# ScalarE's row statistics of tile i+2: behind the transposes of tile i+1, or ahead of the first gelu half of tile i

## The chip, the cores and the metric

The kernel runs on one core of one Trainium2 chip. The metric is the device time of one execution in microseconds. The kernel before was timed three times: 1892.87, 1883.16 and 1890.80 us, median 1890.8 us.

## What is computed

A transformer layer over `x` of 16 sequences x 512 tokens x 256 features, in float32, with three parts that are summed:

```python
xn = layernorm(x)
a  = xn + gdn(layernorm(xn, ln1))          # gated delta rule: a recurrence over the 512 tokens,
                                           # 16 heads of 16 x 16 state per sequence
h  = gelu(layernorm(a, ln2) @ w1 + b1) @ w2 + b2      # w1 256 x 1024, w2 1024 x 256
out = x + (a + h) + moe(xn)                # 64 experts, top 8, plus a shared expert
```

The change touches the order of the middle part's MLP (`h`) on one engine.

## The kernel before, in words

The 8192 tokens are 64 tiles of 128 rows. Five engines run programs of their own, each strictly in the order written in the kernel, tied together by semaphores. The outer loop of all of them is the recurrence: 64 iterations `I` of 8 tokens. VectorE (DVE) does the recurrence, 8 steps `s` = 0 to 7 per iteration, each of two groups of four instructions (lines 1128, 1133, 1137, 1143). GpSimd (POOL) reads out the states, two halves per iteration (lines 822, 830 to 838). TensorE (PE), ScalarE (ACT) and the rest of DVE and POOL do everything else between these.

Iterations 0 to 16 also carry the router and the shared expert, 19 to 34 the experts. From iteration 35 (`FILL`) on comes the MLP, the last 790 us. Iteration 36+n takes tiles 2n and 2n+1 for n below 13; after that two or three tiles (at the end one or two) per iteration. Tiles 0 to 55 are one segment, 56 to 59 the next, 60 to 63 are done behind the recurrence by code of their own. Iterations 36 to 47 (tiles 0 to 23) carry besides one tile `f` of the "front", the q, k, v and gate projections of a later block.

A tile `i` of the MLP goes through these steps:

- `back_attn(i)`, PE lines 1772 and 1773: the attention output times Wo, plus bias.
- `back_x1(i)`, DVE line 1105: adds the residual. It sits at a fixed step of the recurrence: in an iteration with own tiles (a, a+1), tile a+2 at s=2 and tile a+3 at s=6; with three own tiles at s=1, 4 and 6.
- `back_stats(i)`, ACT lines 1454 and 1456: two passes over the row, one for the mean, one for the variance, each followed by a read of the accumulator.
- `back_rstd(i)`, POOL lines 898, 754 and 900: the reciprocal root, at fixed places between POOL's reads; behind it `back_rest`, line 906.
- `back_norm(i)`, ACT line 1462; `back_T(i)`, PE line 1778, the transposes; `back_evac(i)`, ACT line 1468, their copy out of PSUM.
- `back_mid(i, half)`, PE line 1789, 16 matmuls each; `back_gelu(i, half)`, ACT line 1478, four gelus each.
- `back_out(i)`, PE line 1800, 16 matmuls; `back_sum(i)`, DVE line 1112, adds the rest and ends the tile. It too has fixed steps: with two own tiles (a, a+1), tile a-2 at s=0 and tile a-1 at s=4.

The front tile takes `front_norm` (ACT line 1318, `xa`), `front_T` (PE line 1663), `front_evac` (ACT line 1325, `xaT`), `front_qk` and `front_vg` (PE line 1669, then ACT lines 1337 and 1358; 1358 is a sigmoid and needs another activation table than gelu).

PE's order for own tile i is written out as: `back_attn(i+2)`; for the first tile `front_T`; `back_mid(i, 0)`; `back_T(i+1)`; for the second tile `front_vg`; `back_mid(i, 1)`; for the first tile `front_qk`; `back_out(i-1)`. `front_qk` waits for `xaT`, that is for ACT's `front_evac`. `back_mid(i+1, 0)` waits for `back_evac(i+1)` and for the first gelu half of tile i.

ACT's `back_stats(i)` waits for `x1_ready`, that is for DVE's `back_x1(i)`:

```python
act.wait_ge(x1_ready, i + 1)
a_.activation(hb[i % 2], x1[r], ACT.Copy, scale=-1.0 / D, accum_out=ng_b[:, r:r + 1]).then_inc(avg_ready, 1)
act.wait_ge(avg_ready, i + 1)
a_.activation(hb[i % 2], x1[r], ACT.Square, bias=ng_b[:, r:r + 1], accum_out=sq_b[:, r:r + 1]).then_inc(dev_ready, 1)
```

Of the kernel before, what the change touches and what calls it, by code (L numbers as in the profile page):

```python
# [70 lines left out]
def seg_of(i):  # L71
    return max(n for n in range(3) if SEG[n] <= i)


def same_seg(i, k):
    return 0 <= k < NT and seg_of(i) == seg_of(k)
# [16 lines left out]
def refill_at(I):  # L93
    return [i for i in REFILL if REFILL[i] == I]
# [48 lines left out]
def rounds_at(I):  # L143
    if I == R1 + 1:
        return (0, 1)
    return (I - R1,) if R1 + 1 < I < R1 + NR else ()
# [32 lines left out]
def layer(nc, x, Wq, Wk, Wv, Wb, Wg, Wo, bo, ln1_g, ln1_b, ln2_g, ln2_b, w1, b1, w2, b2,  # L179
          router_wT, w_gate, w_up, w_down, ws_gate_up, ws_down, out):  # L180
    ctx = ExitStack()
    with ctx:
# [1120 lines left out]
        def _(act):  # L1303
# [6 lines left out]
            def front_norm(f, i, first=False, behind=0):  # L1310
                if first:
                    act.wait_ge(stats_done, f // NB2 + 1)
                else:
                    act.wait_ge(stats_done, f // NB2 + 1)
                    act.wait_ge(xt_ld[i], (f >> 1) * 16 + 16)
                if behind is not None:
                    act.wait_ge(fT_done, f - behind)
                a_.activation(xa[i], xs[f // NB2][:, f % NB2, :] if first else xt[i], ACT.Identity, scale=sA[:, bass.ds(f, 1)],
                              bias=bA[:, bass.ds(f, 1)]).then_inc(xa_ready, 1)

            def front_evac(f, i, bank=FQ, behind=0):
                act.wait_ge(fT_done, f + 1)
                act.wait_ge(qkv_done, f - behind)
                for c in range(DC):
                    last = a_.activation(xaT[i][:, c, :], bank[:, c * P:(c + 1) * P], ACT.Identity,  # L1325
                                         scale=lncol[:, 0, c:c + 1], bias=lncol[:, 1, c:c + 1])
                last.then_inc(xaT_ready, 1)
# [19 lines left out]
            def front_qk(f, i):  # L1347
                act.wait_ge(qk_done, f - AHEAD * NB2 + 1)
                out_free(f, i)
                for n in range(4):  # L1350
                    last = out_copy(i, n, FQ[:, n * P:(n + 1) * P])
                last.then_inc(qk_out, 1)

            def front_vg(f, i):
                act.wait_ge(qkv_done, f + 1)
                for n in range(4, 6):
                    out_copy(i, n, FQ[:, (n - 4) * P:(n - 3) * P])
                a_.activation(gst[i], FQ[0:2 * H, 2 * P:3 * P], ACT.Sigmoid).then_inc(stg_ready, 1)
# [19 lines left out]
            def stage(L, h):  # L1378
                par, t0 = lookup(L)
                act.wait_ge(prod_done, L * 2)  # L1380
                for s in range(2):
                    act.wait_ge(*window_in(L // NB2, s))
                    last = a_.activation(qs[h][:, :, s, :], win[0][:, par, s, :, bass.ds(t0, ST)].rearrange("p d t -> p t d"),
                                  ACT.Copy)
                last.then_inc(act_staged, 1)
# [10 lines left out]
            def route_exp(I):  # L1396
                act.wait_ge(ld_ready, I + 1)
                act.wait_ge(w_ready, I)
                a_.activation(ex, ld, ACT.Exp).then_inc(e_ready, 1)

            def route_counts(I, half):
                act.wait_ge(mt_done, I * 2 + half + 1)
                act.wait_ge(cum_st[I % 2], I // 2 * 32)
                n = RT * P // 2
                a_.activation(wst[I % 2][:, half * n:(half + 1) * n], YB[0:E, D:D + n], ACT.Copy).then_inc(mT_ready, 1)
# [40 lines left out]
            def back_stats(i):  # L1446

                r = i % 4
                act.wait_ge(x1_ready, i + 1)
                if i >= 2:  # L1450
                    act.wait_ge(hT_done, i - 1)
                if i >= 4:
                    act.wait_ge(nb_ready, i - 3)
# [4 lines that stand above are left out]
            def back_norm(i):  # L1458
                r = i % 4
                act.wait_ge(nb_ready, i + 1)  # L1460
                act.wait_ge(dev_ready, i + 1)
                a_.activation(hb[i % 2], x1[r], ACT.Identity, scale=rs_b[:, r:r + 1], bias=nb_b[:, r:r + 1]).then_inc(hb_ready, 1)

            def back_evac(i):
                act.wait_ge(hT_done, i + 1)
                if i >= 2:
                    act.wait_ge(mid_done, i * 2 - 2)
                a_.activation(hT[i % 2].rearrange("p c t -> p (c t)"), (TB, LG)[i % 2][:, D:2 * D], ACT.Copy).then_inc(hT_ready, 1)

            def back_gelu(i, half):  # L1470
                if i == 0:
                    act.wait_ge(rows_free, 1)
                if i >= 2:
                    act.wait_ge(out_done, i - 1)
                act.wait_ge(mid_done, i * 2 + half + 1)
                for n in range(MC // 2):
                    m = half * (MC // 2) + n
                    last = a_.activation(mid[i % 2][:, m, :], (G0, G1)[half][:, n * P:(n + 1) * P], ACT.Gelu, bias=b1_s[:, m:m + 1])  # L1478
                last.then_inc(gelu_done, 1)
# [39 lines left out]
            def choose(t):  # L1519

                act.wait_ge(pre_used, 1)
                act.wait_ge(slot_mm, t)
                for r in range(RT):
                    for c in range(2):
                        last = a_.activation(oh[:, r, c, :], slot_pm[:, c, :], ACT.Sign, bias=thr2[:, t * RT + r, c:c + 1])
                last.then_inc(onh_ready, 1)
# [38 lines left out]
            def back_iteration(I, h, tiles, f):  # L1565
                if f is not None:
                    front_norm(f, h)
                for b in refill_at(I):
                    back_stats(b)
                    back_stats(b + 1)  # L1570
                    back_norm(b)
                    back_evac(b)
                    back_norm(b + 1)
                for p, i in enumerate(tiles):
                    back_gelu(i, 0)
                    if same_seg(i, i + 1):
                        back_evac(i + 1)
                    if f is not None and p == 0:
                        front_evac(f, h)
                    if f is not None and p == 1:  # L1580
                        front_vg(f, h)
                    if same_seg(i, i + 2):
                        back_stats(i + 2)
                    back_gelu(i, 1)
                    if same_seg(i, i + 2):
                        back_norm(i + 2)
                    if f is not None and p == 0:
                        front_qk(f, h)
                if f is not None and len(tiles) == 1:
                    front_vg(f, h)  # L1590
                if I == FILL:
                    front_evac(f, h)
                    front_qk(f, h)
                    front_vg(f, h)
                    act.wait_ge(mlp_in, 16 * 5)
                    act.wait_ge(mlp_bias, 2)
                    for c in range(DC):
                        a_.activation(w1_s[:, c, :], w1_s[:, c, :], ACT.Copy, scale=lncol[:, 2, c:c + 1]).then_inc(mlp_w, 1)
                    for i in range(2):
                        back_stats(i)  # L1600
                    for i in range(2):
                        back_norm(i)
                    back_evac(0)
                if I < R0 or R1 <= I < X0:
                    front_evac(f, h)
                    front_qk(f, h)
                    front_vg(f, h)
                if I == R1:
                    route_counts(NRT - 1, 0)
                    route_counts(NRT - 1, 1)  # L1610
                    route_exp(NRT - 1)
                if I + 1 < NI:
                    stage(I + 1, 1 - h)
                if I == R1 + 1:
                    for t in rounds_at(I):
                        choose(t)
                        count_up(t)
                    choose(2)

            for I in range(NI):  # L1620
                h, f, i = I % 2, front_of(I), I - R0
# [364 lines left out]
```

## Time and profile before

| | |
|---|---|
| median of three runs | 1890.8 us (1883.16 to 1892.87) |
| profiled execution, its own time | 1887.13 us |
| its span, first to last instruction | 1885.4 us |
| busy: DVE | 1692.1 us (90%) |
| busy: POOL | 1590.8 us (84%) |
| busy: PE matmuls | 1430.0 us (76%) |
| busy: ACT | 911.9 us (48%) |
| mean granted TensorE clock | 0.844 |

DVE is busy nine tenths of the span, and in the MLP phase more than that. Times of single instructions are microseconds from the span's start. A line of a timeline gives start, duration, engine, line, operation, tiles and count, and in brackets how long the engine was idle before it and which instruction ended that; a line of the waits gives the waiting instruction's engine, tile and line, the releaser, the total in us, how often, and the longest.

### The profile page before, as it was taken

The numbers are of one execution on the slowest core, as the hardware profiler recorded it, in microseconds if no ns is written. First come the engines' busy times: TensorE is split into PE (matmuls) and PEld (weight loads), VectorE is DVE, ScalarE is ACT, GpSimd is POOL, SyncE is SP. The second block draws the span as 40 slices with busy tenths as digits, with TensorE's granted clock in tenths as the row PEclk, the third lists the DMA queues.
The fourth block names the chain that finished last, engine by engine and source line by source line (L and its number), as shares of the span: only waits on it lengthen the run. The fifth ranks groups of instructions, "written<-read, shape, count | busy, mean of one in ns | idle before, by whom it ended". The sixth has DMA issues, their size and how long they took to land. (4 is left out here: it accounts for less than half of the span.)

```text
span 1885.4 us, 31540 instructions
## 1 busy us (share of the span) xinstructions
PE 1430.0 (76%) x8846; PEld 1246.3 (66%) x8846; DVE 1692.1 (90%) x4987; ACT 911.9 (48%) x2616; POOL 1590.8 (84%) x1352
## 2 busy tenths in 40 slices
PE   6777778777863666676666658898888989889858
PEld 5666667766752565565555547777777878778757
DVE  3699999999999999999977988999899999999990
ACT  4545555466544555555533345555554445434313
POOL 5279999898998889888897788998899999999861
PEclk9878788778875878887877679999999999999879
DMA  8584334533347567756568422242223311211211
GB/s 183 146 183 114 75 96 113 134 96 97 76 125 172 129 147 174 210 130 164 141 157 221 97 46 55 62 133 81 61 62 104 90 56 53 66 51 48 54 40 28
DMA packets 337170, 201.25 MB, mean 107 GB/s; under 512 B 208226, under 2 KB 327716, under 8 KB 336996
## 3 DMA queue, kind: packets, MB, share of 16 engines
q1 hardware_dynamic: 318724, 168.43, 34.3%
q0 software_dynamic: 15616, 30.55, 7.2%
q8 instruction: 71, 1.16, 0.3%
q14 instruction: 103, 0.84, 0.1%
q10 hardware_dynamic: 2656, 0.26, 0.1%
HBM read 127.58 MB, written 71.60 MB: 106 GB/s over the span
## 5 line engine op out<-in xcount | busy, mean ns | idle before, releaser
L822 POOL TENSOR_TENSOR rp<-S,qs 128x2048 f32<-128x2048 f32 x113 | 521.1, 4612 | 50.6 <-DVE S L1143 36.6
L1143 DVE SCALAR_TENSOR_TENSOR S<-S,gwin,bank 128x256 f32<-128x256 f32 x1024 | 496.5, 485 | 0.3
L1133 DVE TENSOR_REDUCE nu<-vwin 128x16 f32<-128x272 f32 x1024 | 451.6, 441 | 0.3
L1137 DVE TENSOR_TENSOR bank<-nu,bank 128x256 f32<-128x256 f32 x1024 | 443.4, 433 | 0.6
L1128 DVE TENSOR_TENSOR vwin<-S,bank 128x256 f32<-128x256 f32 x1024 | 434.6, 424 | 0.3 <-DVE nu L1133 0.2
L1789 PE MATMUL bank<-region 128*128 128x128 f32 x2048 | 281.3, 296 | 0.0
L830 POOL TENSOR_TENSOR r<-rp 128x1024 f32<-128x1024 f32 x113 | 273.5, 2420 | 7.0
L1789 PEld LDWEIGHTS bank<-region 128*128 128x128 f32 x2048 | 265.6, 209 | 18.5 <-issue 18.1
L1669 PE MATMUL bank<-xaT,wqkvg 128*128 128x128 f32 (+1 forms) x1792 | 241.5, 288 | 11.9 <-ACT xaT L1325 8.6
L1800 PE MATMUL bank<-region 128*128 128x256 f32 x1024 | 235.3, 384 | 0.0
L1669 PEld LDWEIGHTS bank<-xaT,wqkvg 128*128 128x128 f32 (+1 forms) x1792 | 215.7, 190 | 26.4 <-ACT xaT L1325 12.3
L1478 ACT ACTIVATE region<-bank,b_s 128x128 f32<-128x128 f32 x512 | 144.8, 364 | 139.6 <-PE bank L1789 139.4
L1800 PEld LDWEIGHTS bank<-region 128*128 128x128 f32 x1024 | 193.7, 194 | 24.4
L1704 PE MATMUL bank<-gT,region 128*96 128x128 f32 x1024 | 157.8, 319 | 48.1 <-ACT gT L1410 41.7
L1704 PEld LDWEIGHTS bank<-gT,region 128*96 128x96 f32 x1024 | 144.7, 197 | 63.7 <-ACT gT L1410 51.9
L1415 ACT ACTIVATE sgu<-bank 96x256 f32<-96x256 f32 x128 | 48.6, 380 | 218.2 <-PE bank L1704 208.4
L1704 PE MATMUL bank<-gT,wsgu_s 128*96 128x128 f32 x1024 | 152.6, 313 | 0.0
L831 POOL TENSOR_TENSOR r<-r 128x512 f32<-128x512 f32 x113 | 143.7, 1271 | 8.9
L866 POOL DMA_INDIRECT acc_d<-region,idx_i x64 | 101.6, 1588 | 47.6 <-issue 33.8
L1704 PEld LDWEIGHTS bank<-gT,wsgu_s 128*96 128x96 f32 x1024 | 141.5, 195 | 0.0
L1337 ACT ACTIVATE stg<-bank 128x128 f32<-128x128 f32 x384 | 76.6, 281 | 120.5 <-PE bank L1669 110.1
L1694 PE MATMUL bank<-ident,region 128*128 128x128 f32 x256 | 62.4, 334 | 72.1 <-DMA region<-xw_d,idx_i 70.3
(169 smaller groups left out, 2371.8 us busy)
## 6 DMA issues: line engine op xcount, KB each, us to landing
qkv_d<-stg SPq DMA_DIRECT2D x192, 128.0 KB, 2.2
region<-in_L_ffn_w_gate SPq DMA_DIRECT2D x64, 192.0 KB
region<-in_L_ffn_w_up SPq DMA_DIRECT2D x64, 192.0 KB
region<-in_L_ffn_w_down SPq DMA_DIRECT2D x64, 192.0 KB
region<-in_L_attn_x SPq DMA_DIRECT2D x16, 512.0 KB, 7.2
region<-in_L_attn_x SPq DMA_DIRECT2D x32, 256.0 KB, 4.4
xw_d<-region SPq DMA_DIRECT2D x32, 256.0 KB, 3.4
acc_d<-region SPq DMA_DIRECT2D x32, 256.0 KB, 4.1
```

The source lines that it names most:

```text
L822: g.tensor_tensor(rp[:, :, :].rearrange("p (a v) d -> p a v d", v=DH), S[h][:, lo:lo + HS].rearrange("p t s (v d) -> p (t s) v d", v=DH), ...
L830: link(g.tensor_tensor(r1[:, :, :], rp[:, :, 0:8], rp[:, :, 8:16], ALU.add))
L831: link(g.tensor_tensor(r1[:, :, 0:4], r1[:, :, 0:4], r1[:, :, 4:8], ALU.add))
L1128: m[G] = mark(v.tensor_tensor(products_of(I, s, G)[0], earlier(h, s, G).rearrange("p (v d) -> p v d", v=DH), key(I, s, G), ALU.mult))
L1133: m[G] = mark(v.tensor_reduce(nu[:, G], products_of(I, s, G)[1], AX.X, ALU.add))
L1137: m[G] = mark(v.tensor_tensor(outer[G].rearrange("p (v d) -> p v d", v=DH), nu[:, G].unsqueeze(2).to_broadcast([P, DH, DH]), key(L, s, G), ...
L1143: ins = v.scalar_tensor_tensor(S[h][:, s, G], earlier(h, s, G), gwin[:, I // NB2 & 1, G, 1, t:t + 1], outer[G], ALU.mult, ALU.subtract)
L1478: last = a_.activation(mid[i % 2][:, m, :], (G0, G1)[half][:, n * P:(n + 1) * P], ACT.Gelu, bias=b1_s[:, m:m + 1])
L1669: last = mm(dst[0:n, :], wqkvg[:, c, i * P:i * P + n], xaT[h][:, c, :], start=(c == 0), stop=(c == DC - 1))
L1704: last = mm(bk[0:FH, i * P:(i + 1) * P], w[:, c, (i % 2) * FH:(i % 2 + 1) * FH], gT[:, c, :], start=(c == 0), stop=(c == DC - 1))
L1789: last = mm((G0, G1)[half][:, n * P:(n + 1) * P], w1_s[:, c, m * P:(m + 1) * P], hT[i % 2][:, c, :], start=(c == 0), stop=(c == DC - 1))
L1800: last = mm(out_bank(i)[:, 0:D], mid[i % 2][:, m, :], w2_s[:, m, :], start=(m == 0), stop=(m == MC - 1))
```

## The change

In `back_iteration` of ScalarE's program `back_stats(i + 2)` is issued ahead of `back_gelu(i, 0)` instead of ahead of `back_gelu(i, 1)`. It passes the first gelu half, `back_evac(i + 1)` and, where a front tile is carried, `front_evac` (first own tile) or `front_vg` (second own tile). No instruction is added or removed. It holds for tiles i = 0 to 53, 56 and 57; the code behind the recurrence for tiles 60 to 63 keeps its order.

```diff
                 for p, i in enumerate(tiles):
+                    if same_seg(i, i + 2):
+                        back_stats(i + 2)
                     back_gelu(i, 0)
                     if same_seg(i, i + 1):
                         back_evac(i + 1)
@@
                     if f is not None and p == 1:
                         front_vg(f, h)
-                    if same_seg(i, i + 2):
-                        back_stats(i + 2)
                     back_gelu(i, 1)
                     if same_seg(i, i + 2):
                         back_norm(i + 2)
```

## Rows read from the trace of the kernel before

**Rows 1.** The page's part 1: busy time of each engine.
```profile
PE 1430.0 (76%) x8846; PEld 1246.3 (66%) x8846; DVE 1692.1 (90%) x4987; ACT 911.9 (48%) x2616; POOL 1590.8 (84%) x1352
```

**Rows 2.** Busy time by window: length, engines, clock, DMA; with front, then without.
```profile
1111.00:1426.00 315.00, 275.82 (x1703) 240.37 (x1703) 289.46 (x830) 177.94 (x517) 286.49 (x270) 0.93 0.27 75
1426.00:1746.00 320.00, 286.55 (x1685) 248.82 (x1684) 309.46 (x892) 136.25 (x455) 297.68 (x292) 0.94 0.22 67
```

**Rows 3.** Waits of all engines, 1111 to 1426 us, the iterations with a front tile.
```profile
PEld bank L1663 <- ACT xa L1318: 33.2, 11, 6.3
...
DVE region L1112 <- PE bank L1800: 24.3, 7, 8.5
ACT region L1454 <- DVE region L1105: 13.8, 9, 3.0
...
POOL region L898 <- ACT region L1456: 8.5, 5, 2.6
```

**Rows 4.** Waits of all engines, 1426 to 1746 us, the iterations without one.
```profile
ACT region L1462 <- POOL region L900: 105.0, 30, 7.4
ACT region L1454 <- DVE region L1105: 43.3, 18, 4.5
...
DVE region L1112 <- PE bank L1800: 7.5, 5, 3.8
DVE region L1105 <- PE bank L1773: 2.6, 3, 1.0
```

**Rows 5.** Timeline of ACT, 1168 to 1173.5 us: first own tile, number 4.
```profile
1168.76 1.14 ACT L1478 ACTIVATE region<-bank,b_s 128x128 f32<-128x128 f32 x4 [2.38 <-PE bank L1789]
...
1170.04 0.83 ACT L1325 ACTIVATE xaT<-bank,lncol 128x128 f32<-128x128 f32 x2
1172.01 0.42 ACT L1454 ACTIVATE region<-region 128x256 f32<-128x256 f32 x1 [1.14 <-DVE region L1105]
...
1173.06 0.60 ACT L1478 ACTIVATE region<-bank,b_s 128x128 f32<-128x128 f32 x2
```

**Rows 6.** Timeline of PE in the same tile: `front_qk`, then `back_out` of tile 3.
```profile
1170.93 2.05 PE L1669 MATMUL bank<-xaT,wqkvg 128*128 128x128 f32 x16 [0.26 <-ACT xaT L1325]
1172.81 3.62 PE L1800 MATMUL bank<-region 128*128 128x256 f32 x16
```

**Rows 7.** Timeline of DVE: `back_x1` and `back_sum` of iterations 38 and 46; one stall.
```profile
1171.60 0.38 DVE L1105 TENSOR_TENSOR region<-bank,region 128x256 f32<-128x256 f32 x1
...
1177.46 0.43 DVE L1112 TENSOR_TENSOR region<-bank,region 128x256 f32<-128x256 f32 x1
...
1361.54 0.42 DVE L1112 TENSOR_TENSOR region<-bank,region 128x256 f32<-128x256 f32 x1 [6.42 <-PE bank L1800]
...
1380.71 0.37 DVE L1105 TENSOR_TENSOR region<-bank,region 128x256 f32<-128x256 f32 x1
...
1386.57 0.43 DVE L1112 TENSOR_TENSOR region<-bank,region 128x256 f32<-128x256 f32 x1
```

**Rows 8.** DVE's waits, 1166 to 1426 us (own tiles 4 to 23).
```profile
DVE region L1112 <- PE bank L1800: 14.9, 5, 6.4
```

**Rows 9.** Timeline of PE behind a gap, first own tile number 6.
```profile
1193.12 0.69 PE L1663 MATMUL bank<-ident,xa 128*128 128x128 f32 x2 [4.63 <-ACT xa L1318]
1193.60 3.62 PE L1789 MATMUL bank<-region 128*128 128x128 f32 x16
...
1200.08 1.95 PE L1669 MATMUL bank<-xaT,wqkvg 128*128 128x128 f32 x16
1201.86 3.62 PE L1800 MATMUL bank<-region 128*128 128x256 f32 x16
```

**Rows 10.** POOL's waits, 1111 to 1760 us: those for the statistics.
```profile
POOL region L898 <- ACT region L1456: 11.0, 8, 2.6
```

**Rows 11.** Timeline of POOL: one of these waits.
```profile
1475.59 0.19 POOL L898 TENSOR_SCALAR region<-region 128x1 f32<-128x1 f32 x1 [1.91 <-ACT region L1456]
```

**Rows 12.** Timeline of PE: a `back_out` behind another gap.
```profile
1558.87 4.69 PE L1800 MATMUL bank<-region 128*128 128x256 f32 x16
```

## The prediction

> **What bounds the kernel now.** I read the page's busy shares first. DVE is at 90% of the span, POOL at 84%, PE at 76%, ACT at 48% [rows 1]. So ACT, the one engine whose program changes, has time to spare, and the edit adds no work to it; it can only move other engines' waits. The windows say where: with a front tile DVE is busy 289.5 of 315 us, without one 309.5 of 320 [rows 2]. DVE is the bound of both stretches, and what the time consists of besides its work is its idle time, 25.5 us in the first and 10.5 in the second. The waits name it: nearly all of it is DVE sitting in `back_sum` until PE has finished `back_out`, 24.3 us in 7 waits in the first stretch [rows 3], 7.5 and, for `back_x1`, 2.6 us in the second [rows 4]. A stall of `back_sum` stops the recurrence behind it, since DVE runs in order. So the question is: what does the edit do to the moment at which `back_out(i-1)` ends, measured against DVE's fixed steps?
>
> The waits show two more things. POOL waits for the statistics, 11.0 us in 8 waits [rows 10]; that is what an earlier `back_stats` can give back. And ACT itself waits for DVE in `back_stats`: 13.8 us in 9 of the first stretch's 24 tiles, 43.3 us in 18 of the second's [rows 3, 4]. In these tiles `x1` isn't there yet when ACT asks for it, although ACT asks late, behind the gelu. Asking earlier can't bring `x1` earlier. There the edit turns "ACT waits with the gelu done" into "ACT waits with the gelu not begun".
>
> **The change part by part.**
>
> *The statistics themselves* cost 1.05 us of ACT: from line 1454 at 1172.01 to the next gelu at 1173.06 [rows 5]. Before and after the edit they are done once per tile; what is behind them in the new order (first gelu half, `back_evac`, and `front_evac` or `front_vg`) starts that much later unless ACT was idle, and later still if it has to wait for `x1`.
>
> *First own tile with a front tile: a new cycle.* This is the term that decides. On PE `front_qk` stands between `back_mid(i, 1)` and `back_out(i-1)`. It waits for `xaT`, ACT's line 1325, which now stands behind `back_stats(i+2)`. `back_stats(i+2)` waits for `back_x1(i+2)` at DVE's s=2, and DVE's s=4 wants `back_out(i-1)`. Everything on that way is in series:
>
> - `back_x1` ends at 1171.60 + 0.38 = 1171.98 [rows 7]; the gelu behind the statistics starts at 1173.06 [rows 5]: 1.08 us.
> - From the start of that gelu half to the start of `front_qk`: 1168.76 [rows 5] to 1170.93 [rows 6], 2.17 us. It holds four gelus, the copy of the transposes and the two `xaT` instructions. PE waited for just this: 0.26 us, released by line 1325 [rows 6].
> - `front_qk` start to `back_out` start 1.88 us, `back_out` itself 3.62 us [rows 6]: 5.50 us.
>
> Sum 8.75 us. DVE allows from the end of `back_x1` to `back_sum` where nothing stalls 1177.46 - 1171.98 = 5.48 us in iteration 38, and 1386.57 - 1381.08 = 5.49 us in iteration 46 [rows 7]. The difference, 3.3 us, is a stall of DVE in every such iteration. It can't be worked off by running ahead, because the cycle starts at DVE's own step two steps before. In tile 4 now: the gelu starts at 1168.76, 3.2 us before `x1` is there, and `back_out` is done a microsecond before DVE asks. The edit takes exactly this head start away.
>
> It does not add to all the stalls that exist. These sit in the same place, `back_sum` at s=4, and the later of two conditions counts. Of the 12 iterations with a front tile I leave the first two out: the first has no `back_out` before it that is asked for, and the second already stalls 24.3 - 14.9, so over 8 us [rows 3, 8], on a gelu that comes late because of the roots of the gates, with `x1` long there. The other ten have 14.9 us of stalls in five iterations [rows 8]. After the edit: ten times 3.3 = 33 us, and where 6.4 us stand now [rows 7] they stay, being due to that same block boundary work: +3.1. Together 36.1 - 14.9 = **+21.2 us**.
>
> *Second own tile with a front tile.* Its statistics have their `x1` at s=6. The gelu, `front_vg`, two table loads and the second gelu follow, then `back_norm(i+2)`, the next `xa` and `front_T`. This makes `front_T` later, for which PE already waits 33.2 us in 11 waits [rows 3]. But DVE stands still 3.3 us in the same iteration, which moves everything else as well, and from s=6 to the next s=4 there are six steps, about three times 5.5. I take nothing here; bound above is the clock rival below.
>
> *Tiles without a front tile (24 to 53).* There is no `front_qk`, and `back_out(i-1)` needs nothing that passes through the first gelu half of tile i. What comes later is `back_evac(i+1)` and so `back_mid(i+1, 0)`. In its place PE idles now, because the transposes of the tile after wait for `back_norm`, which waits for POOL: 105.0 us in 30 waits [rows 4]. That is the cover, 3.5 us a tile against 1.08 + 1.3 us behind `x1`. If POOL were faster, it would be gone. On the other side the waits of POOL for the statistics can go: 1.91 us at 1475 [rows 11], in a tile whose `x1` is early. It lies on the way to the 3.8 us stall behind it [rows 4]. And POOL, which has to keep up with a slower DVE in the first stretch, comes into the second with less behind. Bounds: 0, and the 7.5 + 2.6 = 10.1 us of stalls that are there [rows 4]. I take **-3 us**, near the one row that shows a gain.
>
> *Nothing else moves.* The statistics issue no DMA and use functions for which the trace shows no table load ahead of them, neither behind the gelu nor behind the sigmoid. Tiles 56 and 57 are followed by pure recurrence of DVE with PE waiting; the last four tiles keep their order.
>
> Total +18 us on the profiled execution's own 1887.1 us: 1905. The median of the runs stands 3.7 us above that execution (1890.8); I put the forecast between the two sums (1905 and 1909): **1907 us**.
>
> **The rivals.**
>
> *A. The statistics were what POOL waited for (faster).* Place: line 898. Price: all 8 waits, 11.0 us [rows 10], give 1876 us on the profiled sum. It decides if `x1` is as a rule ready before the first gelu half could start, so that statistics fill ACT's idle time ahead of it. For it: ACT is idle there, 2.38 us in the row shown [rows 5], and POOL's share is high. Against it: ACT's 27 waits for `x1` [rows 3, 4], and that 8.5 of the 11.0 us lie in the stretch where POOL's delay isn't what DVE waits for. The Trainium skill would have it so: "Perfetto Trace Analysis", section Optimization Strategy, says to find the gaps on the most loaded engine and to make what ends them start sooner. This edit is that rule applied to POOL's gaps.
>
> *B. No change.* DVE's new stalls at s=4 are paid back: the iterations that stall now by 3.8 to 6.4 us do so because PE is behind, and a DVE that was held 3.3 us one iteration before finds PE caught up. Then only 14.9 us or little more stay, and the time is 1887 to 1891. For it: the stalls come in every second iteration now, after one without. Against it: the cycle of 8.75 us begins at DVE's own step, so it is due even with PE caught up completely.
>
> *C. The clock falls as well (slower still).* After a gap of 4.63 us PE's 16 matmuls of `back_mid` took 3.62 us [rows 9] where `front_qk`'s 16 of the same shape take 1.95 to 2.05 [rows 6, 9]; a `back_out` behind a gap took 4.69 [rows 12] instead of 3.62. If the new gap ahead of `front_qk` is as long as that one, the cycle is longer by 1.6 + 1.1 = 2.7 us, ten times: 1905 + 27 = 1932. It decides with the length of that gap: I work out 4.3 us for the first such iteration (1173.06 against 1168.76 for the gelu), but about 1 us later on, since `front_T` then starts later too. The Trainium skill ("TensorE: Matmul & The Clock Gate", section HAM oscillation) warns of this: waits that return in each round of a loop can put the engine back to the low clock each time.
>
> **How the numbers follow.** Forecast 0.62, A 0.12, B 0.13, C 0.13. The low end takes in B down to 1889, the high end most of C, 1928; outside are A and the worst of C. About 0.5% (9.5 us) is what a measurement of this kernel can tell from no change. Slower by more than that: most of the forecast and C, 0.70. Faster: A, 0.11. Within: B, and the part of the forecast in which the second stretch gives back nearly all of its 10 us, 0.19.
>
> **What would show it.** In the profile after: DVE's wait for line 1800 between tiles 4 and 23 at about 36 us in ten waits of 3 us or more instead of 14.9 in 5; PE's line 1669 waiting for `xaT` about 1 to 4 us each time; ACT's line 1454 waiting for DVE ahead of the first gelu half; POOL's wait at line 898 for ACT near zero; the stretch 1426 to 1746 as long as now or a little shorter. I am wrong if the waits of DVE stay at five in those ten iterations, which would be B, or if the second stretch grows, since then the delay of `back_evac` was not covered by `back_norm`.

## The result: slower by 1.07%, and the profile after

The changed kernel takes 1910.3 us (median, 1907.5 to 1912.3), the kernel before 1890.7 in the same comparison: ratio 1.0107, 95% interval 1.0087 to 1.0127. The profiled execution took 1911.2 us with a span of 1909.5, against 1887.13 and 1885.4. So the two profiled executions stand 24.1 us apart where the medians stand 19.7 apart; the traces have to account for the 24.1.

The page's part 1 of the changed kernel, busy time by engine:

```profile
PE 1438.9 (75%) x8846; PEld 1252.8 (66%) x8846; DVE 1692.9 (89%) x4987; ACT 908.5 (48%) x2616; POOL 1591.1 (83%) x1352
```

DVE, POOL and ACT have the work they had [rows 1]; PE has 9 us more for the same 8846 matmuls; nearly all of it lies in the iterations of own tiles 4 to 23 (244.0 us busy instead of 235.2), where the mean granted clock is 0.91 instead of 0.94. What was added is DVE's idle time. DVE's waits in the changed kernel, first own tiles 4 to 23, then the iterations without a front tile to the end of the segment:

```profile
DVE region L1112 <- PE bank L1800: 40.0, 10, 5.8
```
```profile
DVE region L1112 <- PE bank L1800: 6.2, 4, 3.5
DVE region L1105 <- PE bank L1773: 4.5, 5, 1.0
```

The first answers to [rows 8]: 14.9 us in 5 waits have become 40.0 in 10, one in each iteration. The second, 10.7 us together, answers to the 10.1 us of [rows 4] (10.5 to the end of the segment). The account closes: +25.1 us in the ten iterations, +0.4 in the one before them, +0.2 in the second stretch, and -1.7 because this execution came to the first tile 1.7 us earlier, make 24.0 of 24.1.

One ordinary iteration of the changed kernel (own tiles 8 and 9) shows the cycle, DVE, ACT and PE in turn:

```profile
1228.52 0.40 DVE L1105 TENSOR_TENSOR region<-bank,region 128x256 f32<-128x256 f32 x1
...
1237.79 0.42 DVE L1112 TENSOR_TENSOR region<-bank,region 128x256 f32<-128x256 f32 x1 [3.28 <-PE bank L1800]
```
```profile
1228.95 0.42 ACT L1454 ACTIVATE region<-region 128x256 f32<-128x256 f32 x1 [4.92 <-DVE region L1105]
...
1230.00 1.12 ACT L1478 ACTIVATE region<-bank,b_s 128x128 f32<-128x128 f32 x4
1231.00 0.40 ACT L1468 ACTIVATE region<-bank 128x256 f32<-128x256 f32 x1
1231.26 0.83 ACT L1325 ACTIVATE xaT<-bank,lncol 128x128 f32<-128x128 f32 x2
```
```profile
1224.09 0.69 PE L1663 MATMUL bank<-ident,xa 128*128 128x128 f32 x2 [2.89 <-ACT xa L1318]
1224.57 3.62 PE L1789 MATMUL bank<-region 128*128 128x128 f32 x16
...
1228.41 2.48 PE L1789 MATMUL bank<-region 128*128 128x128 f32 x16
1232.15 2.05 PE L1669 MATMUL bank<-xaT,wqkvg 128*128 128x128 f32 x16 [1.26 <-ACT xaT L1325]
1234.04 3.62 PE L1800 MATMUL bank<-region 128*128 128x256 f32 x16
```

ACT idles 4.92 us with nothing to do but wait for `x1`; the gelu, the copy and `xaT` follow at once; PE waits for `xaT` and issues `front_qk` and `back_out` back to back; DVE stands still until `back_out` is done. From the end of `back_x1` (1228.92) to `back_sum` (1237.79) are 8.87 us, 3.28 of them a stall.

PE's rows show one thing more. Behind the gap ahead of `front_T` the granted clock is 0.50 (from 1224.10 to 1228.00), and the first `back_mid` takes 3.62 us. This costs nothing here: PE is still done 1.26 us before `xaT`, and from 1232.15 to 1237.50, in `front_qk` and `back_out`, the clock is 1.00 again.

### The profile page after: what moved, and what is told of

It is laid out like the page before. It is cut to its first block and busy times, and to the rows that moved or that the text cites. A ratio compares the mean times of both kernels' runs of the same rounds, so it can differ in the third digit from the quotient of the medians.

```text
span 1909.5 us, 31540 instructions
## 1 busy us (share of the span) xinstructions
PE 1438.9 (75%) x8846; PEld 1252.8 (66%) x8846; DVE 1692.9 (89%) x4987; ACT 908.5 (48%) x2616; POOL 1591.1 (83%) x1352
## 5 line engine op out<-in xcount | busy, mean ns | idle before, releaser
L1143 DVE SCALAR_TENSOR_TENSOR S<-S,gwin,bank 128x256 f32<-128x256 f32 x1024 | 480.7, 469 | 0.3
L1133 DVE TENSOR_REDUCE nu<-vwin 128x16 f32<-128x272 f32 x1024 | 435.6, 425 | 0.3
L1137 DVE TENSOR_TENSOR bank<-nu,bank 128x256 f32<-128x256 f32 x1024 | 428.4, 418 | 0.6
L1128 DVE TENSOR_TENSOR vwin<-S,bank 128x256 f32<-128x256 f32 x1024 | 419.3, 409 | 0.3 <-DVE nu L1133 0.2
L1789 PE MATMUL bank<-region 128*128 128x128 f32 x2048 | 291.6, 303 | 0.0
L1789 PEld LDWEIGHTS bank<-region 128*128 128x128 f32 x2048 | 276.1, 216 | 20.4 <-issue 20.1
L1669 PE MATMUL bank<-xaT,wqkvg 128*128 128x128 f32 (+1 forms) x1792 | 244.5, 290 | 24.7 <-ACT xaT L1325 21.4
L1800 PEld LDWEIGHTS bank<-region 128*128 128x128 f32 x1024 | 191.5, 192 | 25.0 <-issue 1.3
L1454 ACT ACTIVATE region<-region 128x256 f32<-128x256 f32 x64 | 26.7, 417 | 329.4 <-DVE region L1105 320.9
```

Source lines behind the costliest of these rows:

```text
L1128: m[G] = mark(v.tensor_tensor(products_of(I, s, G)[0], earlier(h, s, G).rearrange("p (v d) -> p v d", v=DH), key(I, s, G), ALU.mult))
L1133: m[G] = mark(v.tensor_reduce(nu[:, G], products_of(I, s, G)[1], AX.X, ALU.add))
L1137: m[G] = mark(v.tensor_tensor(outer[G].rearrange("p (v d) -> p v d", v=DH), nu[:, G].unsqueeze(2).to_broadcast([P, DH, DH]), key(L, s, G), ...
L1143: ins = v.scalar_tensor_tensor(S[h][:, s, G], earlier(h, s, G), gwin[:, I // NB2 & 1, G, 1, t:t + 1], outer[G], ALU.mult, ALU.subtract)
L1669: last = mm(dst[0:n, :], wqkvg[:, c, i * P:i * P + n], xaT[h][:, c, :], start=(c == 0), stop=(c == DC - 1))
L1789: last = mm((G0, G1)[half][:, n * P:(n + 1) * P], w1_s[:, c, m * P:(m + 1) * P], hT[i % 2][:, c, :], start=(c == 0), stop=(c == DC - 1))
```

## Experiments

All ratios are to the kernel before, run on the same chip at the same time (1890.5 to 1890.9 us). "Ten stalls" are DVE's waits for line 1800 at s=4 in the iterations of own tiles 4 to 23: 14.9 us before, 40.0 in the changed kernel.

### Each class of tile alone

In three kernels the statistics go ahead of the gelu for one class of tiles only. The edit, with the condition of the first:

```diff
+                    ahead = f is not None and p == 0
+                    if ahead and same_seg(i, i + 2):
+                        back_stats(i + 2)
                     back_gelu(i, 0)
@@
-                    if same_seg(i, i + 2):
+                    if not ahead and same_seg(i, i + 2):
                         back_stats(i + 2)
```

**First own tile with a front tile.**

> The change made only for the first own tile of iterations with a front tile (12 of the 56 tiles). Theory (cycle over xaT: back_x1 at s=2, statistics, gelu, xaT, front_qk, back_out, back_sum at s=4): it brings the whole loss, 19 to 24 us over the kernel before, about 1912, and DVE's waits for line 1800 in own tiles 4 to 23 stand at 36 to 40 us in ten, as in the changed kernel. Rival (the loss comes through the second own tile, whose later gelu delays back_norm, xa and front_T): under 5 us over before. Rival (low clock of PE does most of it): the stalls vary with the clock, 3 to 6 us, and are not 3.3 us each where the clock is high.

Measured: 1930.8 us, ratio 1.0204 (1.0174 to 1.0234). Twelve tiles cost 40 us, twice what the whole change costs. The place was right, the size was missed by half. DVE's ten stalls and one of them on PE:

```profile
DVE region L1112 <- PE bank L1803: 55.1, 10, 6.2
```
```profile
1234.17 1.95 PE L1792 MATMUL bank<-region 128*128 128x128 f32 x16
1242.59 3.78 PE L1672 MATMUL bank<-xaT,wqkvg 128*128 128x128 f32 x16 [6.46 <-ACT xaT L1325]
1246.16 4.44 PE L1803 MATMUL bank<-region 128*128 128x256 f32 x16
```

(Three lines were added above these, so 1800 is 1803 here.) The gap ahead of `front_qk` is 6.46 us, against 1.26 in the same iteration of the changed kernel, and behind it `front_qk` takes 3.78 us instead of 2.05. The windows of this run give the granted clock of PE ahead of the gap and behind it (columns: length; busy time of PE, weight loads, DVE, ACT, POOL; clock; DMA share; GB/s):

```profile
1233.00:1236.00 3.00, 3.00 (x29) 2.93 (x27) 3.00 (x10) 0.00 (x0) 2.92 (x2) 1.00 0.11 28
1242.50:1246.00 3.50, 3.41 (x16) 3.42 (x17) 2.44 (x7) 1.56 (x6) 3.25 (x3) 0.50 0.76 267
```

From 1.00 to 0.50, from 2.4 to 1.2 GHz. So this stall of 5.80 us is 3.3 us of cycle plus 2.5 of clock. Nine of the ten iterations have a gap of 4.5 us or more there, and behind it a clock of 0.50 to 0.56; the tenth, with a gap of 1.67, keeps 1.00. So the rival of the low clock, second of the two, may hold about half of this loss; the filler below tests it.

**Second own tile with a front tile.**

> The change made only for the second own tile of iterations with a front tile. Theory: 0 to +4 us over the kernel before (1891 to 1895), since the later gelu and front_T only lengthen the stalls that stand there in every second iteration. Rival (second own tile is the cause): +15 us or more.

Measured: 1897.3 us, ratio 1.0032 (1.0014 to 1.0049), ten stalls 23.3 us in 8. Alone it costs 6 us, somewhat more than the 0 to 4 expected, and far from the 15 of the rival. These stalls come by way of `front_T`: in six of the ten iterations `front_qk` doesn't wait for `xaT` at all. Together with the first own tile it saves 20: the whole change is at 1910.3 and the first own tile alone at 1930.8. The reason stands in the PE rows of the two kernels. Where the second own tile's gelu waits too, `front_T` comes later (2.89 us of gap ahead of it at 1224.09), and the low clock falls on `back_mid`, in time that PE would have waited for `xaT` anyway. Where only the first own tile's waits, `front_T` is hardly late:

```profile
1231.89 0.44 PE L1666 MATMUL bank<-ident,xa 128*128 128x128 f32 x2 [0.26 <-ACT xa L1318]
```

Both `back_mid` then run at the high clock, the whole gap stands ahead of `front_qk`, and the low clock falls on the two things DVE is waiting for.

**Tiles without a front tile.**

> The change made only for the tiles without a front tile (24 to 53, 56, 57). The prediction's term for it was -3 us, with POOL's 1.9 us wait at 1475 gone; the trace of the changed kernel shows 10.7 us of DVE waits there where 10.1 stood, so I now expect -2 to +2 us against the kernel before. Rival (the back_evac that comes later costs PE time): +4 us or more.

Measured: 1889.9 us, ratio 0.9997 (0.9983 to 1.0012). No difference that can be told from none; the interval reaches from -3.2 to +2.3 us.

### The clock by itself

The kernel with the first own tile alone gets matmuls without use ahead of `front_qk`, into the gap, from tile 2 on (16 of them) and then from tile 4 on (11, the edit shown). The wait ahead of them keeps them off a bank that DVE has yet to read. Each call shows as two matmuls in the trace, so 16 are x32 and 11 are x22:

```diff
                     if f is not None and p == 0:
+                        if i >= 4:
+                            pe.wait_ge(fin_ready, i - 1)
+                        for _ in range(11 if i >= 4 else 0):
+                            mm(YB[:, 0:D], ident[:, :], wo_s[:, 0, :], start=True, stop=True)
                         front_qk(f, h)
```

> The change made only for the first own tile with a front tile (1930.8), and 16 matmuls of 128x256 without use put on PE ahead of front_qk, into the gap of 6.46 us that stands there. Theory (the low clock behind the gap adds 2.7 us to each of ten stalls on top of the 3.3 us of the cycle): front_qk's 16 matmuls take about 2.0 instead of 3.78 us, the stalls 3.3 to 3.8 us, 33 to 40 us in all instead of 55.1; time 1910 to 1916. Rival (the extra 2.7 us come from another wait): 1928 or more, as PE only gets more work.

Measured with 16: 1927.6 us, ratio 1.0195. By the number the rival (1928) had won. The trace says otherwise:

```profile
1234.47 7.07 PE L1923 MATMUL bank<-wo_s,ident 128*128 128x256 f32 x32
1241.38 1.95 PE L1672 MATMUL bank<-xaT,wqkvg 128*128 128x128 f32 x16
```

`front_qk` is at the high clock, but the filler, 7.07 us, ends after `xaT` is there and makes it late. The stalls are 4.4 us in four of the ten iterations; the ten sum to 49.0 us, 6 less than the 55.1 without filler, and the stall in tile 2's iteration takes these back (14.9 instead of 8.9). The fill was too long; whether it was wrong in kind, the shorter one tests.

> As the kernel with 16 filler matmuls (1927.6), but 11 of them and none in tile 2. In the former the fillers took 7.07 us and ended after xaT was there, so front_qk was warm (1.95 us) but late: stalls of 4.4 us. Eleven take 4.9 us. Theory: front_qk at the high clock and on time, stalls of 3.3 us as in the changed kernel, DVE's waits in own tiles 4 to 23 at 33 to 38 us, time 1908 to 1914, 17 to 22 us under the kernel with the change for the first own tile alone. Rival (fillers can't repair it, the clock isn't the cause): 1926 or more.

Measured with 11: 1910.0 us, ratio 1.0101 (1.0080 to 1.0122): 21 us less than without filler, for more work on PE. DVE's waits, and PE in the filler and behind it:

```profile
DVE region L1112 <- PE bank L1803: 34.3, 10, 4.7
```
```profile
1223.24 4.91 PE L1923 MATMUL bank<-wo_s,ident 128*128 128x256 f32 x22
1229.86 2.05 PE L1672 MATMUL bank<-xaT,wqkvg 128*128 128x128 f32 x16 [1.70 <-ACT xaT L1325]
1231.74 3.62 PE L1803 MATMUL bank<-region 128*128 128x256 f32 x16
```

Nine of the ten stalls are 3.29 us to the hundredth, the tenth (block boundary) is 4.72. The granted clock in `front_qk` and `back_out` is 1.00 in all ten. That is the cycle without the clock; the other 20.8 of the 55.1 us were the clock.

### The cycle's two ends

**`back_x1` one step earlier**, on top of the change:

```diff
-    steps = {1: (2,), 2: (2, 6), 3: (1, 4, 6)}.get(len(own), ())
+    steps = {1: (2,), 2: (1, 6), 3: (1, 4, 6)}.get(len(own), ())
```

> The changed kernel, and DVE's back_x1 of the first own tile at step s=1 instead of s=2 in iterations with two own tiles. Theory (cycle from back_x1 to back_sum): the way of 8.75 us then has 5.5 + 2.8 = 8.3 us, so this cycle costs 0.5 us. Next comes the way over the second own tile: in the changed kernel front_T starts 8.5 us behind back_x1 of s=6, and with front_qk at once behind the second back_mid back_sum could start 20.0 to 20.4 us behind it, against 18.0 us of slot, so about 2.2 us per ordinary iteration; all ten together about 27 us instead of 40.0, time 1895 to 1900. Rival (the place of back_x1 doesn't count): 1908 to 1912 as the changed kernel.

Measured: 1897.9 us, ratio 1.0031 (1.0016 to 1.0045); the ten stalls 24.7 us in 8 (25.5 with a wait of another tile in the window). Nearly two thirds of the loss go with one moved addition of 0.4 us. It isn't all of it, because the way over the second own tile and `front_T` is the next to be late, as expected: in seven of the ten iterations `front_qk` no longer waits for `xaT`.

**The statistics between the two places**, behind the first gelu half and the copy, ahead of `front_evac`:

```diff
                         back_evac(i + 1)
+                    if same_seg(i, i + 2):
+                        back_stats(i + 2)
                     if f is not None and p == 0:
                         front_evac(f, h)
@@
-                    if same_seg(i, i + 2):
-                        back_stats(i + 2)
                     back_gelu(i, 1)
```

> The kernel before with back_stats(i+2) behind back_evac(i+1) but ahead of front_evac or front_vg: behind the first gelu half, unlike in the change. The gelu (1.0 us) and the copy (0.26) leave the way, so 7.5 us against 5.5 us of slot: 2.0 us per iteration at the high clock. But now the second tile's gelu doesn't wait, front_T comes early as in the run with the first own tile alone, and the gap is all ahead of front_qk; if it is over 4 us the low clock adds 2.7 us. Theory with the clock: DVE's waits in own tiles 4 to 23 at 40 to 48 us in ten, 1912 to 1920. Without the clock: 22 to 27 us, 1898 to 1904. Rival (gelu's own place is what counts, not xaT's): as before, 1888 to 1894.

Measured: 1902.7 us, ratio 1.0067 (1.0047 to 1.0086), the ten stalls 30.1 us. It lies between the two expectations, and its rows show why. Two of its iterations, `front_qk` and the stall of each:

```profile
1231.66 3.30 PE L1669 MATMUL bank<-xaT,wqkvg 128*128 128x128 f32 x16 [3.81 <-ACT xaT L1325]
```
```profile
1259.60 2.05 PE L1669 MATMUL bank<-xaT,wqkvg 128*128 128x128 f32 x16 [1.28 <-ACT xaT L1325]
```
```profile
1238.94 0.42 DVE L1112 TENSOR_TENSOR region<-bank,region 128x256 f32<-128x256 f32 x1 [3.62 <-PE bank L1800]
```
```profile
1265.25 0.43 DVE L1112 TENSOR_TENSOR region<-bank,region 128x256 f32<-128x256 f32 x1 [1.98 <-PE bank L1800]
```

Where the gap is 1.28 us the stall is 1.98, the 2.0 of the working; where it is 3.81 `front_qk` takes 3.30 us, the granted clock is 0.58, and the stall is 3.62. Five of the ten stalls are 1.98 to 2.02 us; in four others `front_qk` is slowed. The rival that only gelu's place counts is out: gelu came first here.

**PE's order.** `front_qk` behind `back_out(i-1)`, once on the changed kernel, once on the kernel before:

```diff
+                    if same_seg(i, i - 1):
+                        back_out(i - 1)
                     if f is not None and p == 0:
                         front_qk(f, h)
-                    if same_seg(i, i - 1):
-                        back_out(i - 1)
```

> The changed kernel, and in PE's order front_qk issued behind back_out(i-1) instead of ahead of it. Theory: back_out no longer waits for xaT, the 5.50 us behind xaT shrink to nothing for back_sum, and the stalls of 3.3 us go; what stays is the chain from back_x1 at s=6 over back_norm, xa, front_T and both back_mid, worked out at 18.5 us against 18.0: 0.5 to 1 us in an ordinary iteration, more at the two block boundaries. DVE's waits in own tiles 4 to 23 under 15 us; time 1884 to 1892. Rival (the loss is not tied to front_qk's place): 1905 or more.

> The kernel before, with PE's front_qk behind back_out(i-1) as in the run where this was done to the changed kernel (1878.5). It takes 1.9 us from each of the five stalls in own tiles 4 to 23 and from that of tile 1: DVE's waits there from 14.9 to 5 to 8 us, time 1880 to 1885. Theory 1: the gain of 12 us is that of PE's order alone, so this kernel is at 1875 to 1883. Theory 2: part of it is from the earlier statistics once xaT no longer stands in the way; then this kernel is slower than 1883.

Measured: the changed kernel with this order 1878.5 us, ratio 0.9927 (0.9900 to 0.9954); the kernel before with it 1885.7 us, ratio 0.9976 (0.9961 to 0.9990). The first is below both kernels, by 32 us under the changed one, and below the 1884 to 1892 expected. The ten stalls are 8.5 us in the first and 13.7 in the second; tile 2's, which is not among them, is 2.6 in both. So the second missed its expectation of 5 to 8 us of stalls: without the earlier statistics PE's order alone takes little from them. The rival of the first, that the loss isn't tied to `front_qk`'s place, is out. In the second, theory 2 holds: once `xaT` stands in nobody's way, the earlier statistics are worth something, the 7 us between the two. POOL's waits for the statistics in the kernel before with this order:

```profile
POOL region L898 <- ACT region L1456: 11.6, 5, 3.9
```

and in the changed kernel with it:

```profile
POOL region L898 <- ACT region L1456: 1.0, 2, 0.6
```

These waits, 11.0 us in the kernel before [rows 10], are gone.

### Which tiles bring that gain

Both kernels have `front_qk` behind `back_out(i-1)`; one keeps the old place of the statistics for the first own tile with a front tile, the other for the second.

> front_qk behind back_out(i-1), and the statistics ahead of the gelu for every tile but the first own tile of an iteration with a front tile. Theory (what the earlier statistics give in the kernel with this PE order, 1878.5 against 1885.7, comes from the first own tile, whose x1 is there long before a gelu that comes late at a block boundary, so that POOL doesn't wait and is ahead afterwards): none of it here, 1883 to 1890. Rival (it comes from the second own tile or the tiles without a front tile): 1876 to 1881.

> front_qk behind back_out(i-1), and the statistics ahead of the gelu for every tile but the second own tile of an iteration with a front tile. Theory as in the run beside it (the first own tile gives the gain): 1874 to 1880. Rival: 1883 to 1888.

Measured: 1886.5 us (0.9968, 0.9945 to 0.9990) without the first own tile, 1882.3 (0.9953, 0.9936 to 0.9971) without the second; the ten stalls 11.4 and 10.2 us. Left without the first own tile, the gain is gone (1885.7 without any of the earlier statistics), as expected; that the first gives all of it is not borne out, since 1882.3 lies between the ranges. With both classes the stalls are 8.5 us. The intervals of the two kernels overlap, and that of the second also overlaps the 0.9961 to 0.9990 of the kernel with none; so how the gain divides stays open.

**Both remedies at once**, `front_qk` behind `back_out` and `back_x1` at s=1:

> The changed kernel with both remedies: front_qk behind back_out(i-1) and back_x1 of the first own tile at s=1. If what is left of the stalls (8.5 us in four, own tiles 4 to 23) still hangs on x1 of the first own tile: 1870 to 1876. If it hangs on the way over the second own tile and the block boundaries, as I think: no change against front_qk's move alone, 1876 to 1881.

Measured: 1877.8 us, ratio 0.9927 (0.9898 to 0.9955), the same as with the changed kernel and PE's order alone (1878.5). With the order changed, `x1` of the first own tile no longer sets the time.

## Why the prediction was right

**What bounds the kernel.** Right. DVE's work is the same to 1 us, and the difference of the two spans is that of its waits, up to the 1.7 us by which this execution came earlier to the first tile.

**The cycle of the first own tile.** Right in place and mechanism, and nearly in size. Worked out 8.75 us against 5.48 of slot, a stall of 3.3; in the changed kernel 8.87 us against 5.59, and stalls of 3.28 and 3.29 in five of the ten iterations. Predicted for the ten 36.1 us, measured 40.0. What the sum missed is mostly PE's clock. The first of the ten iterations has 5.36 instead of 3.3, with a gap on PE:

```profile
1173.95 3.78 PE L1669 MATMUL bank<-xaT,wqkvg 128*128 128x128 f32 x16 [4.68 <-ACT xaT L1325]
```

This is rival C, which I had worked out for just this iteration (4.3 us of gap) and left out of the sum. The last of the ten, 4.95, is the same on a smaller scale:

```profile
1429.58 2.62 PE L1669 MATMUL bank<-xaT,wqkvg 128*128 128x128 f32 x16 [2.90 <-ACT xaT L1325]
1431.99 4.77 PE L1800 MATMUL bank<-region 128*128 128x256 f32 x16
```

`front_qk` and `back_out` take 0.57 and 1.15 us more than in the ordinary iteration, which makes the 1.66 us over 3.29. Two more, at tiles 13 and 15, stall 3.94 and 3.47. There `front_qk` does not wait for `xaT`: `front_T` came behind a gap of 3.85 and 3.84 us, the `back_mid` behind it ran at a clock of 0.50, and PE was later than `xaT`. That is the way over the second own tile, which I had taken at nothing. The one at the block boundary has 5.83 where I kept 6.4. Together +2.1, +1.7, +0.8 and -0.6 are the 3.9 us.

**The second own tile: taken at nothing.** The step of the prediction that was wrong in kind, though the total hides it. Alone it costs 6 us, and with the first it saves 20, since it decides where PE's gap lies and what runs at the low clock behind it. I had seen that `front_T` would be later and had used it to expect a gap of about 1 us ahead of `front_qk` (it is 0 to 1.3 in six of the ten iterations, 1.5 to 2.9 in three, 4.68 in the first), but booked this as a reason against rival C, not as a saving on which the forecast rested. Whoever had made the change in the first own tile alone, believing the rest neutral, would have lost 40 us.

**Tiles without a front tile: -3 us.** Not seen, and not excluded: +0.2 us in the trace of the changed kernel; for these tiles alone a ratio of 0.9997, whose interval still holds 3 us, and a trace with 8.1 us of DVE's waits there. But the traces of six kernels that keep the old place in these tiles have 8.6 to 11.3 us, so one trace can't show 3. The cover for the later `back_evac` held, as argued. The row that I took the 3 us from belongs to one execution more than to the kernel: I had put POOL's wait of 1.91 us (for tile 30) on the way to the 3.8 us stall (tile 35), which comes 88 us later. In the traces of the five others that keep the old place here this wait is 0 to 1.2 us and the stall at tile 35 is 0.3 to 1.7. So that both are gone in the changed kernel is no gain of the change, and another stall, of 3.54 us, turned up at tile 41. It stands there in the three kernels built on the changed one by moving `back_x1`, PE's order or both (3.56 to 3.63), and not where only these tiles were changed (1.98). Why was not tried.

**Rival A, faster,** is out for this kernel, and with it what the rule of the Trainium skill ("Perfetto Trace Analysis", section Optimization Strategy) would have given here: POOL's gaps were to end sooner, and POOL wasn't what DVE waited for. The rule speaks of the most loaded engine, which was DVE; it was I who turned it on POOL. My sign for it was wrong as well. I expected POOL's wait for ACT near zero; between 1111 and 1785 us of the changed kernel it is longer than the 11.0 us of [rows 10]:

```profile
POOL region L898 <- ACT region L1456: 19.2, 9, 5.1
```

All nine lie in the iterations with a front tile: POOL now catches up with a DVE that stalls, and then waits for `x1` by way of ACT. The wait moved from one cause to another. With PE's order changed there is a gain of rival A's kind: POOL's waits go from 11.6 to 1.0 us, and the time is 1878.5 against 1885.7. That the one makes the other was not tested by itself.

**Rival B, no change,** is out: the stalls stand in every iteration, not paid back by the next.

**Rival C, the clock,** is a small part of what the change costs. In the changed kernel the low clock slows `front_qk` or `back_out` in two of the ten iterations, 3.7 us in all; behind `front_T` it falls in others too, mostly in time that PE would have waited. In the kernel with the first own tile alone it is half of the cost, 21 of 40 us, shown by filling the gap. Here the sentence of the Trainium skill that I set beside it ("TensorE: Matmul & The Clock Gate", section HAM oscillation) agrees with the run: a wait that returned in each of ten rounds put PE back to a clock of 0.50 to 0.56 in the nine where it was 4.5 us or longer.

**The total.** +18 us predicted on the profiled execution, 24.1 measured there, 19.7 between the medians. Of the forecast's closeness to the median (1907 against 1910) some is luck: the -3 that did not come and the 3.9 missed in the ten iterations add up to 7 us, both the same way, and the medians stand 4.4 us nearer together than the two profiled executions. That the second own tile could be taken at nothing is luck too: with the first own tile alone the kernel takes 1930.8 us, above the 1928 at which the range ends.

## What to carry to other kernels

An instruction put ahead of others on an idle engine is not free if it can wait: everything behind it inherits the wait. Look for the instruction it passes whose result another engine's queue is blocked on, and measure the whole way from the event it waits for to the event the bounding engine asks for; if that is longer than the slot between the two, the difference is paid in every round. And test the parts of a change singly, but don't add them up: here one part cost 40 us, another 6, and both together 20.

## What the runs showed of the hardware

That matmuls without use can make a kernel faster, I had not expected in this size: eleven of them ahead of `front_qk` in ten iterations took 21 us off, by keeping the granted clock at 1.00 where it had been 0.50 (`front_qk` 2.05 instead of 3.78 us, `back_out` 3.62 instead of 4.44). A low clock costs only where it falls: in the changed kernel 3.62 us of `back_mid` at a clock of 0.50 cost nothing, because PE had to wait behind them anyway.

Of the gaps seen ahead of `front_qk`, those of 1.26 to 1.99 us left the clock at 1.00, those of 4.53 us and more were followed by 0.50 to 0.56. Between them the length did not decide alone. In the changed kernel one of 2.45 us left the clock high and one of 2.90 was followed by 0.75 (1429.60 to 1432.20); ahead of `front_T` gaps of 2.89 to 2.91 were followed by 0.50 to 0.62 in five iterations and by 1.00 in one. In the kernel with the statistics between the two places gaps of 2.92, 3.53 and 3.81 us, under the 4 us of its expectation, were followed by 0.54, 0.70 and 0.58, and one of 2.09 by 0.51 (`front_qk` 3.68 us), where the `back_mid` ahead of the gap had itself run at 0.72.
